# The last batch's output product inside its last attention unit, with key tiles 4 to 7 as separate terms of the denominator

## What is computed

```
h = maximum(layernorm(x), 0)
q, k, v = h @ Wq + bq, h @ Wk + bk, h @ Wv + bv        # 16 heads of 32
scores = (q @ k.T) / sqrt(32), and -inf where adj == 0
out = x + (softmax(scores) @ v) @ Wo + bo
```

## Time and profile before

| | us |
|---|---|
| median of 3 runs | 1985.43 |
| the three runs | 1985.43, 1992.27, 1981.20 |
| the profiled execution | 1990.77 |
| its span | 1989.0 |
| TensorE busy | 1862.3 |
| GpSimd busy | 1603.2 |
| VectorE busy | 1537.3 |
| ScalarE busy | 1472.6 |
| first masked tile of unit 30, of unit 31, starts at | 1834.4, 1888.4 |

### The profile page before, as it was taken

One profiled execution on the slowest core, in us unless ns is written; L12 is line 12 of the kernel. 1 busy time (PEld: TensorE's weight loads), 2 busy tenths in 40 slices (PEclk: granted clock), 3 DMA queues, 4 the chain that ended last, 5 costly groups with the idle time before them and its releaser, 6 DMA issues.

```text
span 1989.0 us, 35056 instructions
## 1 busy us (share of the span) xinstructions
PE 1862.3 (94%) x13824; PEld 768.7 (39%) x13824; DVE 1537.3 (77%) x1587; ACT 1472.6 (74%) x1765; POOL 1603.2 (81%) x709
## 2 busy tenths in 40 slices
PE   3789999999999899999999999999999999999976
PEld 2333433344343343444433443334434344344312
DVE  5589877788778887688777888778877888767871
ACT  3577887688867688678886788768886788867760
POOL 0478888888798698888898788888879888887983
PEclk8899999999999999999999999999999999999997
DMA  5504344323544136342361434432444323523202
GB/s 178 162 27 107 96 128 133 90 70 107 135 125 116 44 97 159 97 138 77 95 165 54 123 91 133 124 95 74 106 128 133 109 73 95 152 78 80 64 1 86
DMA packets 112392, 206.08 MB, mean 104 GB/s; under 512 B 12640, under 2 KB 12768, under 8 KB 112224
## 3 DMA queue, kind: packets, MB, share of 16 engines
q1 hardware_dynamic: 112224, 203.81, 37.0%
HBM read 153.43 MB, written 50.33 MB: 102 GB/s over the span
## 4 chain that ended last, share of the span: by engine, by line
PE 74%; DVE 10%; DMA 5%; issue 4%; ACT 3%; POOL 1%; SPq 1%; DVEq 0%; POOLq 0%; ACTq 0%
PE ps L708 20%; PE ps L695 19%; PE ps L668 13%; DVE ring L918 8%; PE ps L719 8%; PE ps L682 7%; PE ps L675 7%; DMA k_stack<-k_parts 3%; DMA k_parts<-k_part 1%; ACT ring L783 1%; POOL acc L1094 1%; DMA edges<-adjT 1%; DVE oT_lo L975 1%; PE ps L664 1%; POOL acc L1102 0%
## 5 line engine op out<-in xcount | busy, mean ns | idle before, releaser
L918 DVE TENSOR_TENSOR ring<-ps,mask 128x1024 f32<-128x1024 f32 x1024 | 1217.2, 1217 | 343.3 <-PE ps L695 312.8
L783 ACT ACTIVATE ring<-ring 128x1024 f32<-128x1024 f32 x1024 | 1061.6, 1050 | 234.8 <-DVE ring L918 223.7
L1094 POOL TENSOR_TENSOR acc<-acc,ring 128x1024 f32<-128x1024 f32 x384 | 910.5, 2398 | 2.0 <-ACT ring L783 2.0
L1094 POOL TENSOR_TENSOR acc<-ring 128x1024 f32<-128x1024 f32 x256 | 616.9, 2421 | 352.4 <-ACT ring L783 348.1
L695 PE MATMUL ps<-q_stack,k_stack 128*128 128x512 f16 x2048 | 609.4, 383 | 75.1 <-DVE ring L918 55.3
L708 PE MATMUL ps<-ring,v_sb 128*32 128x512 f32 x4096 | 506.8, 601 | 0.0
L695 PEld LDWEIGHTS ps<-q_stack,k_stack 128*128 128x128 f16 x2048 | 157.6, 98 | 444.0 <-DVE ring L918 248.8
L708 PEld LDWEIGHTS ps<-ring,v_sb 128*32 128x32 f32 x4096 | 107.3, 109 | 263.9 <-issue 234.4
L719 PE MATMUL ps<-acc,ones 128*32 128x512 f32 x1024 | 134.3, 596 | 5.3 <-POOL acc L1094 5.3
L811 ACT ACTIVATE rden<-ps 128x512 f32<-128x512 f32 x64 | 38.3, 598 | 114.8 <-PE ps L719 114.8
L838 ACT ACTIVATE mask<-edges,big 128x512 bf16<-128x512 uint32 x120 | 85.2, 710 | 21.0 <-DMA edges<-adjT 21.0
(11 more groups left out here) (80 smaller groups left out, 1547.7 us busy)
## 6 DMA issues: line engine op xcount, KB each, us to landing
x_in<-x SPq DMA_DIRECT2D x168, 256.0 KB, 2.8
edges<-adjT SPq DMA_DIRECT2D x128, 256.0 KB, 3.1
q_stack<-q_parts SPq DMA_DIRECT2D x128, 256.0 KB, 4.6
k_stack<-k_parts SPq DMA_DIRECT2D x128, 256.0 KB, 4.9
q_parts<-q_part SPq DMA_DIRECT2D x64, 256.0 KB, 2.0
k_parts<-k_part SPq DMA_DIRECT2D x64, 256.0 KB, 2.6
out<-x_in SPq DMA_DIRECT2D x56, 256.0 KB, 2.1
ring<-x SPq DMA_DIRECT2D x2, 1024.0 KB, 6.9
```

What stands on the lines that cost most here:

```text
L783: nc.scalar.activation(tile, tile, ACT.Exp, scale=SCALE / UP / UP).then_inc(s["prob_ready"], 1)
L918: nc.vector.tensor_tensor(ring[:, slot_of(kt, pair), :].rearrange("p (a n) -> p a n", n=HALF), ps_s(j), mask[:, kt:kt + 1, half * HALF:(ha ...
L1094: nc.gpsimd.tensor_tensor(acc[:, group, pair, :], first_of, ring[:, slot_of(kt, pair), :], ALU.add).then_inc(s["sum_done"], 1)
```

## The change

In the last batch the product y is divided. `LAST_Y` places its pieces at the tiles of the last unit, and `last_y_run` issues them:

- for tokens 512 to 1023 (tiles 4 to 7) the "part": the 9 products over the first three units' heads, at tiles 1 to 24. VectorE adds each to its tile of x (`add_last`). The three products over the last unit's heads, the "rest", come at the very end.
- for tokens 0 to 511 (tiles 0 to 3) all 12 products, at tiles 25 to 31 for three of them and behind the last denominator for the fourth. For this the last unit's oT is split by halves of the tokens (`o_high_last`, `o_low_last`): the first half at tiles 22 and 24, the second at the end.

The last batch's rows of x no longer go to `acc`. Tiles 4 to 7 go to the slots of `x_in` as these come free behind the y of the batch before, and tiles 0 to 3 in one transfer of 1 MB to the space of hT_hi, issued at tile 1 of the last unit. GpSimd adds bo to them at the places of `LAST_BIAS_AT`: two tiles in the last batch's second unit and six in its last.

In the two sweeps of the last unit the terms of the denominator are A, 4, 5, 6, 7: GpSimd no longer adds key tiles 4 to 6, and TensorE multiplies these tiles of the ring by ones itself. The slots of the ring are then free when TensorE has read them. The blocks of the last sweep that stood at 18 stand at 16 and 17, with nothing between.

The steps of the flag are taken into the last unit: VectorE's at tiles 3, 20, 24 and 26, GpSimd's reduction over the partitions at tile 12.

```
+LAST_SWEEP = B * UNITS * SWEEPS - 1
+LAST_Y = {("part", 4): ((1, 0, 3), (3, 3, 6), (8, 6, 9)), ("part", 5): ((4, 0, 3), (5, 3, 5), (7, 5, 6), (9, 6, 9)),
+          ("part", 6): ((12, 0, 3), (13, 3, 6), (15, 6, 9)), ("part", 7): ((17, 0, 2), (20, 2, 4), (21, 4, 6), (23, 6, 8), (24, 8, 9)),
+          ("y", 0): ((25, 0, 6), (27, 6, 12)), ("y", 1): ((28, 0, 6), (29, 6, 12)), ("y", 2): ((31, 0, 12),), ("y", 3): ((TILES, 0, 12),)}
+LAST_BIAS_AT = {(1, 24): 4, (1, 25): 5, (3, 8): 6, (3, 9): 7, (3, 14): 0, (3, 15): 1, (3, 24): 2, (3, 25): 3}
+LAST_TERMS = "A4567"
+UNIT_BLOCKS = {6: ("p0", "p1"), 10: ("p2", "p3"), 14: ("p4", "p5", "dA", "d4", "d5"), 18: ("p6", "d6", "p7", "d7")}
+LAST_BLOCKS = {6: ("p0", "p1"), 10: ("p2", "p3"), 14: ("p4", "p5", "dA", "d4", "d5"), 16: ("p6", "d6"), 17: ("p7", "d7")}
...
         def x_last(t):
-            return acc[:, t // 4, t // 2 % 2, t % 2 * D:(t % 2 + 1) * D]
+            return hT_hi[:].rearrange("p c s -> p (c s)").bitcast(F32)[:, t * D:(t + 1) * D] if t < QT // 2 else x_in[:, t % X_SLOTS, :]
...
-                            elif not last:
-                                load_x(g + 1, t + X_SLOTS - QT)
+                            else:
+                                load_x(*((g, t) if last else (g + 1, t + X_SLOTS - QT)))
...
+                        if last and up == UNITS - 1:
+                            if j == 1:
+                                sp.wait_ge(s["chunk_ready"], len(PRO_CHUNKS) + len(SEQUENCE))
+                                sp.dma_start(hT_hi[:].rearrange("p c s -> p (c s)").bitcast(F32).rearrange("p (c d) -> p c d", d=D),
+                                             x_t[b, 0:QT // 2].rearrange("t p d -> p t d")).then_inc(s["x_last"], 16)
+                            for t in range(2):
+                                if LAST_Y["y", t][-1][0] == j - 2:
+                                    sp.wait_ge(s["y_ready"], b * QT + t + 1)
+                                    sp.dma_start(out_t[b, t], x_last(t)).then_inc(stored[t % X_SLOTS], 16)
...
-            for half in range(2):
-                sp.wait_ge(s["den_done"], len(TERMS) * B * UNITS * SWEEPS)
-                sp.dma_start(acc[:, half].rearrange("p a (c d) -> p (a c) d", d=D),
-                             x_t[B - 1, QT // 2 * half:QT // 2 * (half + 1)].rearrange("t p d -> p t d")).then_inc(x_last_loaded[half], 16)
-            for t in range(QT):
+            for t in range(2, QT):
...
+            def last_y(what, t, a, z, bank):
+                order = {"y": range(3 * DC), "part": [m for m in range(3 * DC) if m % DC < 2] + [m for m in range(3 * DC) if m % DC == 2], "rest": [m for m in range(3 * DC) if m % DC == DC - 1]}[what]
+                for n in range(a, z):
+                    k, c = divmod(order[n], DC)
+                    w, o = ((w_hi, oT_hi), (w_lo, oT_hi), (w_hi, oT_lo))[k]
+                    i = nc.tensor.matmul(bank, o[:, c, t * P:(t + 1) * P], w[WO][:, c, :], start=n == 0, stop=n == len(order) - 1)
+                return i
+            def last_y_run(n, what, t, piece, to):
+                if piece == 0:
+                    pe.wait_ge(s["o_ready"], B * UNITS if what == "y" else B * UNITS - 2)
+                    if n < 2:
+                        bank_free(SEQUENCE[n - 2])
+                    elif n < 6:
+                        pe.wait_ge(s["part_added"], n - 1)
+                    else:
+                        pe.wait_ge(s["y_ready"], (B - 1) * QT + n - 5)
+                if what == "part" and to > 6:
+                    pe.wait_ge(s["o_ready"], B * UNITS - 1)
+                i = last_y(what, t, piece, to, ps[:, BANK_M + (len(SEQUENCE) + n) % 2, :])
+                if to == (3 * DC if what == "y" else 3 * (DC - 1)):
+                    i.then_inc(s["chunk_ready"], 1)
...
-            pe.wait_ge(s["o_ready"], UNITS * B)
-            for t in range(QT):
-                products("y", t, 0, 0, PIECES["y"], ps[:, t, :], None).then_inc(s["chunk_ready"], 1)
+            last_y_run(QT - 1, "y", 3, 0, 3 * DC)
+            pe.wait_ge(s["o_ready"], UNITS * B + 1)
+            for t in range(QT // 2, QT):
+                last_y("rest", t, 0, 3, ps[:, t - QT // 2, :]).then_inc(s["chunk_ready"], 1)
...
+                        if last and up == UNITS - 1:
+                            if j == SWEEP + SCALE_O_AT + 3:
+                                o_low_last(0)
+                            for n, (what, t) in enumerate(LAST_Y):
+                                if LAST_Y[what, t][-1][0] == j - 1:
+                                    add_last(n, what, t)
+                            if j in (3, 20, 24, 26):
+                                verdict((3, 20, 24, 26).index(j))
...
+            add_last(QT - 2, "y", 2)
             scale_o(U, 1)
-            o_low(U, UNITS - 1)
...
+            o_low_last(1)
+            add_last(QT - 1, "y", 3)
+            for t in range(QT // 2, QT):
+                add_last(QT + t - QT // 2, "rest", t)
...
+                        if last and (up, j) in LAST_BIAS_AT:
+                            bias_x(b, first, b, LAST_BIAS_AT[up, j])
+                        if last and up == UNITS - 1:
+                            if j == 12:
+                                pool.wait_ge(s["limits_ready"], 6)
+                                nc.gpsimd.partition_all_reduce(limits[:, 0:LIM_QK], limits[:, 0:LIM_QK], P, RMAX).then_inc(s["limits_everywhere"], 1)
+                        if last and up == UNITS - 1 and j % SWEEP // PAIRS >= 4:
+                            continue
```

More of the change, by code:

```diff
@@ L719, in denominators @@
                     i = nc.tensor.matmul(ps[h * DH:(h + 1) * DH, BANK_D, :], ones[:], head_of(tile, h),
-                                         start=term == TERMS[0], stop=term == TERMS[-1], tile_position=(0, h * DH))
+                                         start=term == terms[0], stop=term == terms[-1], tile_position=(0, h * DH))
                 i.then_inc(s["den_done"], 1)
             def blocks(U, up, half, r, very_first):
-                for what, which in BLOCKS.get(r, ()):
+                for what, which in blocks_of(U * SWEEPS + half).get(r, ()):
                     if what == "p":
@@ L745, in graph @@
                             chunk(*run)
+                        if last and up == UNITS - 1:
+                            for n, (what, t) in enumerate(LAST_Y):
+                                for at, piece, to in LAST_Y[what, t]:
+                                    if at == j:
+                                        last_y_run(n, what, t, piece, to)
             pe.wait_ge(s["const_loaded"], 16 * 6)
@@ new lines, in add_last @@
+            def add_last(n, what, t):
+                dve.wait_ge(s["chunk_ready"], len(PRO_CHUNKS) + len(SEQUENCE) + n + 1)
+                if what == "rest":
+                    dve.wait_ge(s["part_added"], t - QT // 2 + 1)
+                else:
+                    dve.wait_ge(s["x_biased"], (B - 1) * QT + 1 + list(LAST_BIAS_AT.values()).index(t))
+                bank = ps[:, t - QT // 2, :] if what == "rest" else ps[:, BANK_M + (len(SEQUENCE) + n) % 2, :]
+                i = nc.vector.scalar_tensor_tensor(out=x_last(t), in0=bank, scalar=1 / UP / UP, in1=x_last(t), op0=ALU.mult, op1=ALU.add)
+                if what == "part":
+                    i.then_inc(s["part_added"], 1)
+                else:
+                    i.then_inc(s["y_ready"], 1)
@@ L1085, in sums @@
                 V = U * SWEEPS + half
-                group, n = kt // 4, SUMS * V + SUMMED[kt] + pair
+                group, n = kt // 4, sums_before(V) + SUMMED[kt] + pair
                 pool.wait_ge(s["prob_ready"], U * TILES + j + 1)
```

88 lines of the change are left out of this document (54 added, 34 removed).

## The result

The changed kernel takes 1966.72 us in the median of six runs (1964.08 to 1972.86), the kernel before 1983.88 in its six (1980.71 to 1992.27). The ratio is 0.9911, with a 95% interval of 0.9885 to 0.9936: about 17.7 us faster, between 12.7 and 22.8. Forecast were 1963.8 us and a gain of 21.6, with a range of 1954 to 1974. A second set of runs of the same kernel gave 0.9903 (0.9875 to 0.9930).

A forecast was written before the change was run, and what follows sets the result against it. TensorE, busy 94%, bounds the batches; the gain lies in the last 50 us. D -0.3, D to L -1.0, L to Y -20.6, Y to the end +0.3 sum to -21.6 on the median 1985.43: 1963.8 us, range 1954 to 1974.

The forecast's parts named there:

- L to Y: From the end of the last oT_lo to the end of the last addition of y: 3.55 us, worth -20.6 us.
- D to L: From the end of the last denominator to that of the last oT_lo: 3.55 us, 4.6 before, worth -1.0 us.
- D: End of the last denominator: 1952.1 us, 1952.4 before, worth -0.3 us.
- Y to the end: From the last addition of y to the span's end: 2.3 plus 5.85 us, worth +0.3 us.
- The walk: Tile-by-tile timing of the last unit: tile 16 at 1917.0 us, 20 at 1924.65, 24 at 1930.15, last denominator at 1952.1.
- the all-reduce: GpSimd's reduction at tile 12 of the last unit: one switch, under 11.7 us of cover, cost 0.
- The five-block group: Block p4 p5 dA d4 d5 ahead of tile 16: 4.5 us where three blocks take 2.8, starving VectorE.
- The clock: TensorE's granted clock in the last unit: kept at full, as a y piece breaks the idle stretch near tile 10.
- Rival 1: GpSimd's switch around its reduction is long or comes twice: 1964 to 1977 us; chance 0.14.
- Rival 2: Last unit packs better than the walk: total -25 to -28.3, 1957 to 1960.5 us; chance 0.10.
- Rival 3: TensorE's clock falls to half at the five-block group and stays: +15, 2000.8 us; chance 0.03.
- Rival 4: The end is not shortened, last stores or last x late by over 12 us: 1975 to 1985 us; chance 0.05.

The follow-up runs named there:

- e8: Changed kernel with all 96 products of the last y behind the last oT_lo: end at 99.90 us from the last unit's first masked tile; ratio 1.0015 to before.
- e1: Changed kernel with the reduction and the flag's last three steps moved to the end: last Ln at 67.84 us, end at 83.22, from the last unit's first masked tile.
- e2: Changed kernel with only the flag's last three steps moved to the last scaling: last Ln at 65.24 us, end at 72.31 plus stores, 80.37.
- e5: Changed kernel with GpSimd's sums of tiles 4 to 6 kept, reduction and flag's last three steps late: last Ln at 65.68 us, end at 85.06.
- e12: e5 with the flag's last three steps behind the last addition of y: end at 80.99 us from the last unit's first masked tile; ratio 0.9894 to before.
- e4: Kernel before with the last unit's separate denominator terms alone: end at 95.70 us from the last unit's first masked tile (before 100.65); ratio 0.9991.
- e3: Changed kernel with a second GpSimd reduction behind the row addition of tile 15: last Ln at 81.33 us, end at 96.23, from the last unit's first masked tile.

## Why the prediction was right, point by point

**The place of the gain** was right and is shown: 19.0 of the 19.7 us come with the placing of the products (e8 against the changed kernel). The forecast for the same sum was 21.6. In whole runs the gain is about 17.7 us, with an interval of 12.7 to 22.8, which can't tell 19.7 from 21.6.

**L to Y** was forecast at 3.55 us and is 3.55. VectorE sets it with five additions, at the full clock. **D to L** was forecast at 3.55 from D, and from the Ln to L it is 3.52. The estimates for the half-size instructions (0.67 and 0.75) measured 0.72 and 0.75. **Y to the end** was forecast at 8.15 and is 8.04.

**D** is the term that was mis-sized. The walk had it 0.3 us ahead of before, and the Ln came 1.7 us later (65.83 for 64.16, 66.34 in the second profile). This 2.0 us is the whole miss of the marks. Most of the walk held: tile 8 at 1897.31 for 1897.3 (the walk's time less the 6.0 us between the profiles), tile 16 at 1911.13 for 1911.0, tile 20 at 1918.99 for 1918.65. Tile 24 came at 1925.87 for 1924.15. In between stands the flag's step of 1.28 us; the walk names no price for the two steps at tile 20 and goes from tile 20 to 24 by TensorE's block alone. Behind tile 24 the half-size oT_lo has 0.65 in the sum and shows 0.89 (0.75 with GpSimd idle). In the second profile the same lateness has other terms: the wait of 1.25 us for GpSimd's sum, and 1.63 us of oT_lo. So two of the walk's prices were too low. VectorE's small instructions were costed as if GpSimd stood idle, though the row of 2.32 us for oT_lo, beside 1.28 at the end, had shown the price. And the all-reduce was put at 0. Moving the steps does not simply give it back, as e1 and e2 show. The remaining 0.3 us ahead of tile 20 I can't assign to a row.

**The five-block group** starves VectorE, as said: 3.51 us idle ahead of tile 16. **The clock** was kept, as taken: 1.00 in every window of the unit, in both profiles. That this was not certain is shown by e1, where it fell behind a wait of 1.81 us, and by e8. Waits as long left it at 1.00 in e5 and e12, so the runs give no length from which on a wait costs it. The waits of the changed kernel were 1.37 us at most. The prediction's reason, that the piece of part 4 breaks the idle stretch, is borne out in the main: in the ten profiles with the pieces the longest wait near tile 10 is 1.36 or 1.37 us, and the clock there is 1.00. In the three without them TensorE waits 2.70 to 2.72 us for the scores of tile 10, and the p blocks behind that wait take 3.64 us in before, 3.04 in e4 and the 1.92 of the full clock in e8. So the clock does not fall behind such a wait each time.

**Rival 1**, GpSimd's switch, happened in its mechanism: idle stretches there and back, 13.0 us. The prediction had taken one switch at a cost of 0. Its price was small and not nil, and that it was small is partly luck: 13.0 to 13.5 us stood against a cover of 11.7, which was a little understated. In the first profile nobody waits for GpSimd. In the second a mask does, for 1.25 us, behind a gap of over 12 us around tile 12, which is what the prediction gave as its first sign of being wrong. e3 shows the price when the cover is gone, 15.5 us. The Trainium skill (GPSIMD Engine Reference, section 2.1 Instruction dispatch) gives some 6 us for the first call of a freshly loaded kernel. The 5.4 to 6.2 us ahead of the reduction agree with it; the way back took 6.7 to 7.6 here. **Rival 2** fell: the unit was not packed better than the walk. **Rival 3** did not occur in the changed kernel. **Rival 4** did not: 8.04 us from Y to the end, for 8.15, and no wait for x.

**A part that I read wrongly without harm**: the prediction names the fetch of x, 6.03 us, and the sums as parts of what is gained. e8 shows the early x to be worth nothing by itself, and e12 that the separate terms are worth nothing beside the products. It was without harm since the sum was taken from D, L and Y and not from these parts.

## What to carry to other kernels

An end of 25 us in which one engine works and the others are idle is worth more than any wait inside a full unit: split what it computes into the part that needs the last result and the part that doesn't, and lay the second into the waits of the unit before it. Before adding an edit to such a change, try it with the others in place: two edits that fill the same wait are worth what one is. A GpSimd reduction of 0.44 us in the middle of its adds cost 13 to 14 us of that engine, so it belongs where GpSimd has that long to spare; and VectorE instructions with operands in SBUF are to be priced with GpSimd running. Take a second profile before putting a miss of 1 or 2 us down to one row: the first one showed a long step, the second a late sum, and the time lost was nearly the same.

## What the runs showed of the hardware that I had not expected

- GpSimd stands idle at each use of the reduction, both ways: 5.4 to 6.2 us ahead of it (eleven profiles; in before and e4 the reduction waits for the norms, and the stretch can't be told from that) and, where GpSimd had more additions to do, 6.7 to 7.6 behind it (six profiles, seven times).
- oT_lo on 512 tokens takes 0.75 us with GpSimd idle and 0.89 to 2.51 by where in a sum of GpSimd it starts; it ends 0.55 us behind that sum, and the next sum takes 2.8 us for 2.35. A VectorE instruction of 0.16 us on 4 elements takes 1.28 us when it starts together with a row addition of GpSimd.
- TensorE's granted clock fell to a mean of 0.57 over 4 us around the end of a wait of 1.81 us (e1), and stayed at 1.00 around waits of 1.82 and 1.80 us at the same place, with the same work of 5.56 or 5.57 in 6.00 us ahead of the wait (e5, e12).
- The last unit started at 1882.36 and at 1886.14 us in two executions of the same kernel, while the unit ahead of it took 53.93 to 53.95 us in all thirteen profiles.
